# DLRM interaction kernel: 16 by-hand gathers, w_tri loaded amid SP's first rows, the last output in two halves

## What is computed

```python
x = jax.nn.relu(dense_features @ W0 + b0)
x = jax.nn.relu(x @ W1 + b1)
dense_out = jax.nn.relu(x @ W2 + b2)
emb = jax.vmap(lambda t, idx: t[idx], in_axes=(0, 1), out_axes=1)(tables, sparse_features)
gram = jnp.einsum('bid,bjd->bij', emb, emb)
interact = gram[:, TRIU_I, TRIU_J]
features = jnp.concatenate([dense_out, interact], axis=1)
return features @ Wt + bt
```

## Time and profile before

| what | us |
|---|---|
| median of 3 runs | 523.09 |
| lowest and highest | 522.91, 523.14 |
| the profiled execution's own time | 523.56 |
| its span, first to last instruction | 521.5 |
| POOL busy | 381.4 |
| PE busy | 304.8 |
| DVE busy | 246.6 |
| ACT busy | 19.2 |

### The profile page before, as it was taken

The page is one execution under the profiler, slowest core; times in us unless marked ns, Lnnn a source line. Parts: engine busy times, 40 slices in busy tenths (PEclk is TensorE's granted clock), DMA queues, the critical chain, the costliest instruction groups (busy, mean ns, idle before and its releaser), DMA issues.

```text
span 521.5 us, 8547 instructions
## 1 busy us (share of the span) xinstructions
PE 304.8 (58%) x1752; PEld 242.1 (46%) x1752; DVE 246.6 (47%) x635; ACT 19.2 (4%) x53; POOL 381.4 (73%) x409
## 2 busy tenths in 40 slices
PE   2814761668576776857577083270734683814697
PEld 1504551547454664746456062250623562713585
DVE  4255533436566374555736345162461865331532
ACT  2000000000000000000000000000000000210312
POOL 5777777777777777777777777777777777777770
PEclk9965575776796776767778557585575757665769
DMA  7212224232232222322222222232222222121110
GB/s 112 28 29 28 31 47 94 30 37 29 38 29 38 29 30 37 31 37 30 38 29 29 37 29 38 29 38 28 31 36 28 40 27 37 27 37 26 38 35 14
DMA packets 24945, 18.74 MB, mean 36 GB/s; under 512 B 14615, under 2 KB 18425, under 8 KB 24876
## 3 DMA queue, kind: packets, MB, share of 16 engines
q0 software_dynamic: 12864, 13.20, 17.8%
q1 hardware_dynamic: 6100, 2.46, 4.8%
q10 hardware_dynamic: 5930, 2.55, 4.4%
HBM read 15.25 MB, written 2.10 MB: 33 GB/s over the span
## 4 chain that ended last, share of the span: by engine, by line
POOL 38%; issue 16%; PE 16%; DVE 13%; SPq 10%; DMA 5%; POOLq 0%; DVEq 0%
POOL emb L321 34%; DVE gram L235 8%; SPq L251 6%; PE mlp_ps L584 6%; PE gram_ps L659 5%; POOL emb L345 4%; DMA w_tri<-in_L_rec_Wt_dram 3%; DVE h L422 2%; PE mlp_ps L671 2%; DVE embT L212 2%; SPq L245 2%; SPq L285 1%; DMA w_gram<-w_tri 1%; PE rowsT_ps L635 1%; PE mlp_ps L591 1%
## 5 line engine op out<-in xcount | busy, mean ns | idle before, releaser
L321 POOL DMA_INDIRECT emb<-in_L_rec_tables_dram,row_idx x376 | 356.0, 947 | 117.7 <-issue 114.2
L235 DVE COPY gram<-gram_ps 32x96 f32<-32x96 f32 x464 | 150.3, 324 | 98.2 <-PE gram_ps L659 92.4
L635 PE MATMUL rowsT_ps<-ident,emb 128*128 128x128 f32 x188 | 36.9, 330 | 122.5 <-DMA emb<-in_L_rec_tables_dram,row_idx 109.7
L659 PE MATMUL gram_ps<-embT 64*128 64x100 f32 x1024 | 92.9, 350 | 23.0 <-DVE gram L235 10.4
L659 PEld LDWEIGHTS gram_ps<-embT 64*128 64x128 f32 x1024 | 86.9, 259 | 32.3 <-issue 32.3
L635 PEld LDWEIGHTS rowsT_ps<-ident,emb 128*128 128x128 f32 x188 | 24.4, 164 | 134.2 <-issue 133.4
L212 DVE COPY embT<-rowsT_ps 128x512 f32<-128x512 f32 (+1 forms) x60 | 47.7, 851 | 74.7 <-PE rowsT_ps L635 74.3
L671 PE MATMUL mlp_ps<-w_gram,gram 128*128 128x256 f32 x224 | 70.6, 483 | 0.1
L584 PE MATMUL mlp_ps<-h,w_sb 128*128 128x256 f32 x128 | 48.7, 562 | 34.3 <-DVE h L422 34.3
L671 PEld LDWEIGHTS mlp_ps<-w_gram,gram 128*128 128x128 f32 x224 | 58.5, 262 | 13.6 <-issue 0.5
L584 PEld LDWEIGHTS mlp_ps<-h,w_sb 128*128 128x128 f32 x128 | 37.3, 299 | 46.7 <-DVE h L422 38.5
(11 more groups left out here) (38 smaller groups left out, 45.0 us busy)
## 6 DMA issues: line engine op xcount, KB each, us to landing
by_hand<-in_L_rec_tables_dram SPq DMA_DIRECT2D x896, 0.2 KB
by_hand<-in_L_rec_tables_dram ACTq DMA_DIRECT2D x896, 0.2 KB
emb<-in_L_rec_tables_dram,row_idx POOLq DMA_INDIRECT x378, 3.4
out_dram<-out_sb ACTq DMA_DIRECT2D x16, 128.0 KB, 8.7
w_gram<-w_tri SPq DMA_DIRECT2D x3, 192.0 KB
w_sb<-in_L_rec_W_dram SPq DMA_DIRECT2D x1, 512.0 KB
emb<-in_L_rec_tables_dram,last_idx POOLq DMA_INDIRECT x24, 2.5
raw_idx<-n_r_sparse_features_dram SPq DMA_DIRECT2D x2, 182.0 KB, 4.2
```

The costliest lines, as they stand in the source:

```text
L235: last = copy(by_quad[FP * g:FP * (g + 1), t0:NS, :, half * HG:(half + 1) * HG, s], gram_ps[FP * s:FP * (s + 1), :, :, src:src + SQ * (NS ...
L321: nc.gpsimd.indirect_dma_start(emb[:, m % PR, k, u, :], None, tables_v[:, :], bass.IndirectOffsetOnAxis(ap=row_idx[:, u, m, k:k + 1], axis=0),
L635: last = nc.tensor.transpose(rowsT_ps[c % 2][:, k - ks.start, :, :], rows.rearrange("p u e -> p (u e)"), ident[:, :])
L659: last = nc.tensor.matmul(gram_ps[:, u, a, 0:SQ * (F - 1)], samples.rearrange("p s f -> p (s f)"), samples[:, :, 1:F], start=True, stop=True)
```

## The change

Pair 14 is added to BY_HAND, so eight pairs have 16 gathers by hand in all. SP loads w_tri after the first 64 of pair 2's rows instead of after all 128. SP_ONLY is empty, so the code that asks for it does nothing.

The last pair's output is made in two halves of 64 samples. `gram_evac` lays the last pair's halves side by side, and the last round of the dense layers writes its output in the same order, in two relu instructions. `top_first_half` forms the first half's output ahead of `last_transposes(3)`; DVE copies it out and ACT stores it in two transfers. `top_last_half` forms the second half's: slots 4 to 6 go into PSUM partitions 64 to 127 of one buffer, the dense part and slots 0 to 3 into partitions 0 to 63 of the other, in turn. ACT copies the former out, DVE adds the two, SP and ACT store 32 rows each. The spare products are set anew: four ahead of `last_transposes(2)`, two ahead of `last_transposes(5)`, five after the last Gram products.

```diff
-    BY_HAND = [2, 4, 5, 7, 9, 10, 12]
+    BY_HAND = [2, 4, 5, 7, 9, 10, 12, 14]
+    SP_ONLY = []
...
-    SPARE = [4, 3, 5]
+    SPARE = [4, 2, 5]
+    SPLIT = 4
     def gathered(m, c):
-        return 2 * len([k for k in CHUNKS[c] if k != HAND_K or m not in BY_HAND])
+        return 2 * len([k for k in CHUNKS[c] if k != HAND_K or m not in BY_HAND]) + (c == LAST and m in SP_ONLY)
...
+    out_last = out.rearrange("(u h r t) o -> h u r t o", u=2, h=2, t=NP)
...
         def gram_evac(copy, blocks, m, half):
-            by_quad = gram[:, m % 2, :, :].rearrange("p t (u a s) -> p t u a s", u=2, s=SQ)
+            if m == LAST_PAIR:
+                by_quad = gram[:, m % 2, :, half * US:(half + 1) * US].rearrange("p t (u a s) -> p t u a s", u=2, s=SQ)
+            else:
+                by_quad = gram[:, m % 2, :, :].rearrange("p t (u h a s) -> p t h u a s", u=2, h=2, s=SQ)[:, :, half]
             for s, g in blocks:
...
-                    by_quad[FP * g:FP * (g + 1), t0:NS, :, half * HG:(half + 1) * HG, s],
+                    by_quad[FP * g:FP * (g + 1), t0:NS, :, :, s],
...
             sp.dma_start(wd_sb[H2:H2 + 1, :], bt.rearrange("(a n) -> a n", a=1)).then_inc(w_top_in, 16)
             sp.wait_ge(hand_idx_ready, 1)
-            fetch_rows(sp, 0, BY_HAND[0], 0, P)
+            fetch_rows(sp, 0, BY_HAND[0], 0, US)
             sp.wait_ge(tri_zeroed, 1)
             for i in range(F - 1):
                 n = F - 1 - i
                 sp.dma_start(w_tri[i:i + 1, i:F - 1, :],
                              wt[tri_row(i):tri_row(i) + n, :].rearrange("(a j) n -> a j n", a=1)).then_inc(tri_in, 16)
+            fetch_rows(sp, 0, BY_HAND[0], US, P)
             sp.wait_ge(tri_in, 16 * (F - 1))
             for g in range(SQ):
                 t0 = first_slot(g)
...
                              w_tri[:, col(t0, g) - 1:F - 1:SQ, :]).then_inc(w_top_in, 16)
             for m in BY_HAND[1:]:
                 fetch_rows(sp, 0, m, 0, P)
-            for q in range(2):
-                sp.wait_ge(stored[q], 16 * ROUNDS)
+            sp.wait_ge(out_ready[1], ROUNDS + 1)
+            sp.dma_start(out_last[1, 0, :, LAST_PAIR, :], tail_sb[0:HS, 1, :]).then_inc(stored[1], 16)
+            sp.wait_ge(stored[0], 16 * ROUNDS)
+            sp.wait_ge(stored[1], 16 * (ROUNDS + 3))
         @block.gpsimd
         def _(pool):
...
             def l2_evac(r):
                 dve.wait_ge(l2_in_psum, r + 1)
-                relu(h2[0:H2, r, :], mlp_ps[1][0:H2, 0:RS], b2_sb[:, 0:1]).then_inc(h2_ready, 1)
+                if r < ROUNDS - 1:
+                    relu(h2[0:H2, r, :], mlp_ps[1][0:H2, 0:RS], b2_sb[:, 0:1]).then_inc(h2_ready, 1)
+                    return
+                relu(h2[0:H2, r, 0:P], mlp_ps[1][0:H2, 0:P], b2_sb[:, 0:1])
+                relu(h2[0:H2, r, P:RS].rearrange("p (h u s) -> p h u s", h=2, u=2),
+                     mlp_ps[1][0:H2, P:RS].rearrange("p (u h s) -> p h u s", h=2, u=2), b2_sb[:, 0:1]
+                     ).then_inc(h2_ready, 1)
...
             gram_blocks(LAST_PAIR, 0)
             out_evac(LAST_PAIR - 1)
+            dve.wait_ge(top_in_psum[1], ROUNDS)
+            dve.wait_ge(stored[1], 16 * (ROUNDS - 1))
+            nc.vector.tensor_copy(out_sb[0:US, 1, :], mlp_ps[1][0:US, 0:NO]).then_inc(out_ready[1], 1)
             for i in range(HALF_DONE[0], HALF_DONE[1]):
...
             gram_blocks(LAST_PAIR, 1)
-            out_evac(LAST_PAIR)
+            dve.wait_ge(top_in_psum[1], ROUNDS + 1)
+            dve.wait_ge(tail_part_ready, 1)
+            nc.vector.tensor_tensor(tail_sb[:, 1, :], mlp_ps[1][0:US, 0:NO], tail_sb[:, 0, :], ALU.add
+                                    ).then_inc(out_ready[1], 1)
         @block.scalar
         def _(act):
...
                     gram_evac(nc.scalar.copy, ACT_BLOCKS, m, half).then_inc(gram_tail_act, 1)
                     if half == 0 and m == LAST_PAIR:
                         store(m - 1)
+                        act.wait_ge(out_ready[1], ROUNDS)
+                        for u in range(2):
+                            act.dma_start(out_last[0, u, :, LAST_PAIR, :], out_sb[u * HS:(u + 1) * HS, 1, :]).then_inc(
+                                stored[1], 16)
                 if m < LAST_PAIR:
                     store(m - 1)
-            store(LAST_PAIR)
+            act.wait_ge(tail_top_in_psum, 1)
+            nc.scalar.copy(tail_sb[:, 0, :], mlp_ps[0][US:P, 0:NO]).then_inc(tail_part_ready, 1)
+            act.wait_ge(out_ready[1], ROUNDS + 1)
+            act.dma_start(out_last[1, 1, :, LAST_PAIR, :], tail_sb[HS:US, 1, :]).then_inc(stored[1], 16)
         @block.tensor
         def _(pe):
...
-            def spare(n):
-                pe.wait_ge(out_ready[(LAST_PAIR - 1) % 2], (LAST_PAIR - 1) // 2 + 1)
+            def spare(n, m):
+                pe.wait_ge(out_ready[m % 2], m // 2 + 1)
                 for _ in range(n):
-                    nc.tensor.matmul(mlp_ps[(LAST_PAIR - 1) % 2][:, 0:NO], ident[:, :], w_gram[:, 0, :], start=True, stop=True)
+                    nc.tensor.matmul(mlp_ps[m % 2][:, 0:NO], ident[:, :], w_gram[:, 0, :], start=True, stop=True)
...
                                             start=False, stop=(t == NS - 1))
                 last.then_inc(top_in_psum[q], 1)
+            def half_of(samples, half):
+                return samples[:, half * US:(half + 1) * US]
+            def top_first_half():
+                nc.tensor.matmul(mlp_ps[1][0:US, 0:NO], half_of(h2[:, ROUNDS - 1, P:2 * P], 0), wd_sb[:, :],
+                                 start=True, stop=False)
+                blocks_out(2 * LAST_PAIR + 1)
+                for t in range(NS):
+                    last = nc.tensor.matmul(mlp_ps[1][0:US, 0:NO], half_of(gram[:, 1, t, :], 0), w_gram[:, t, :],
+                                            start=False, stop=(t == NS - 1))
+                last.then_inc(top_in_psum[1], 1)
+            def top_last_half():
+                pe.wait_ge(out_ready[1], ROUNDS)
+                nc.tensor.matmul(mlp_ps[1][0:US, 0:NO], half_of(h2[:, ROUNDS - 1, P:2 * P], 1), wd_sb[:, :],
+                                 start=True, stop=False)
+                blocks_out(2 * LAST_PAIR + 2)
+                for t in range(SPLIT):
+                    if SPLIT + t < NS:
+                        last = nc.tensor.matmul(mlp_ps[0][US:P, 0:NO], half_of(gram[:, 1, SPLIT + t, :], 1),
+                                                w_gram[:, SPLIT + t, :], start=(t == 0), stop=(SPLIT + t == NS - 1))
+                        if SPLIT + t == NS - 1:
+                            last.then_inc(tail_top_in_psum, 1)
+                    last = nc.tensor.matmul(mlp_ps[1][0:US, 0:NO], half_of(gram[:, 1, t, :], 1), w_gram[:, t, :],
+                                            start=False, stop=(t == SPLIT - 1))
+                last.then_inc(top_in_psum[1], 1)
...
-            for i in range(HALF_DONE[0]):
-                last_transposes(i)
+            last_transposes(0)
+            last_transposes(1)
+            spare(SPARE[0], LAST_PAIR - 3)
+            last_transposes(2)
             gram_products(LAST_PAIR, 0)
             top(LAST_PAIR - 1)
+            top_first_half()
             last_transposes(3)
-            spare(SPARE[0])
             last_transposes(4)
-            spare(SPARE[1])
+            spare(SPARE[1], LAST_PAIR - 1)
             last_transposes(5)
             gram_products(LAST_PAIR, 1)
-            spare(SPARE[2])
-            top(LAST_PAIR)
+            spare(SPARE[2], LAST_PAIR - 1)
+            top_last_half()
```

More of the change, by code:

```diff
@@ L151, in bass_dlrm_forward @@
         out_sb = sb("out_sb", [P, 2, NO])
+        tail_sb = sb("tail_sb", [US, 2, NO])
         rowsT_ps = [pb(f"rowsT_ps_{i}", [P, 4, 2, US]) for i in range(2)]
@@ L198, in bass_dlrm_forward @@
         out_ready = [sem(f"out_ready_{q}") for q in range(2)]
+        tail_top_in_psum = sem("tail_top_in_psum")
+        tail_part_ready = sem("tail_part_ready")
         stored = [sem(f"stored_{q}") for q in range(2)]
@@ L317, in gather @@
                     for k in ks:
+                        if k == HAND_K and m in SP_ONLY:
+                            nc.gpsimd.indirect_dma_start(
+                                by_hand[:, BY_HAND.index(m), 1, :], None, tables_v[:, :],
+                                bass.IndirectOffsetOnAxis(ap=row_idx[:, 1, m, k:k + 1], axis=0),
+                            ).then_inc(rows_in[m % PR][c], 16)
                         if k == HAND_K and m in BY_HAND:
@@ L524, in store @@
                 act.dma_start(out_v[:, m:m + 1, :], out_sb[:, m % 2:m % 2 + 1, :]).then_inc(stored[m % 2], 16)
-            pieces = [(m, c0) for m in BY_HAND for c0 in range(0, P, LOADED)]
+            pieces = [(m, c0) for m in BY_HAND if m not in SP_ONLY for c0 in range(0, P, LOADED)]
             act.wait_ge(hand_idx_ready, 1)
@@ L626, in transposes @@
                     if own:
-                        for u in range(2):
```

(4 more changed lines are left out.)

## The result

The kernel after takes 519.76 us in the median of four runs (519.16, 519.27, 520.25 and 521.84); before, beside it, took 523.12. The ratio is 0.9946 with a 95% interval of 0.9932 to 0.9961: half a per cent faster, which is clear of the noise. The two medians lie 3.4 us apart; the ratio stands for 2.8 us. The forecast was 520.4 in a range of 519.2 to 522.4, and a gain of 2.7. The runs lie wider apart than those of before (2.7 us against 0.4).

The account below looks back on a forecast made before the run. POOL's count of gathers and what follows the last were taken as the whole time. Span 521.5 less 2.50 and 1.06, plus 0.85 for the clock, gave 518.8; 2.7 off the 523.09 median gave 520.4, range 519.2 to 522.4.

Parts of the forecast that it names:

- Two gathers less: On POOL: 400 gathers instead of 402 at 1.25 us each, the last one 2.50 us sooner, at 504.53.
- The halves side by side: In the last slots: records of two column halves run beside each other, 2.20 us instead of 3.26, 1.06 saved.
- The clock: On PE: a fall at about the last Gram products in most executions, 1.71 us whole, taken as 0.85; chance 0.36.
- (c): Rival on PE: clock falls ahead of the last products and stays low through ten spare records, +2.6 us, time 522.1; chance 0.15.
- (a): Rival on PE: the clock holds at its high level, span 517.94, time 519.5; chance 0.24.
- The first half's output ahead of last_transposes(3): On PE: 16 records, 3.4 us, put ahead of those transposes without delaying the last products, 1.7 us to spare.
- F: On PE: the time when the first half's output ends, forecast at 503.7; the last products could follow 2.7 us later.
- The sum of halves: On DVE: adding the two column halves takes 0.42 us, as the copy it replaces, bounds 0.35 to 0.50.
- w_tri: Loads amid SP's rows of pair 2: PE's 11.2 us wait for w_gram goes, but the end gains nothing.
- the rows are wanted at 477 and land by 442. Cost: nothing: Pair 14's 128 rows each on SP and ACT land in time; ACT's end near 439, with 10 us to spare.
- slack 1.7 us, cost nothing: Before the last products: PE is ready at 506.4, the last rows allow them at 508.11, so the early output costs nothing.
- rival (e): On PE: the first half's products become the path; low clock throughout gives +6.8 us, time 526.3; chance 0.05.

Follow-up runs that it names:

- e6_tail: After with pair 14 taken out of BY_HAND again, so POOL makes 402 gathers and the new tail stays; 522.99 us, ratio 0.9994 to before.
- e3_hold: After with five instead of two spare products ahead of last_transposes(5); 520.92 us, ratio 0.9968 to before.
- e2_sequence: e3_hold with all seven last slots in sequence in one half and a plain copy by DVE; 522.41 us, ratio 0.9993 to before.
- a2_after: After measured again without any edit, on another chip; 521.15 us over 7 runs, ratio 0.9963 to before.
- e11_odd: After with pair 14's u = 1 rows gathered by POOL again (401 gathers, 1920 rows); 520.68 us, ratio 0.9964 to before.
- e5_tri: After with SP loading w_tri behind all 128 rows of pair 2, as in before; 520.71 us, ratio 0.9958 to before.
- e10_split: After with each row described as 2 x 128 bytes, though the rows went out whole; 519.93 us, ratio 0.9951 to before.
- e4_fall: After with no spare products ahead of last_transposes(5) instead of two; 522.21 us, ratio 0.9984 to before.
- e9_spares: After with six and four spare products ahead of last_transposes(2) and last_transposes(5) instead of four and two; 520.64 us, ratio 0.9946 to before.
- e1_gathers: Before with pair 14 added to BY_HAND and nothing else; 522.91 us, ratio 1.0003 to before.

## Why the prediction was right

**The sum.** Three measurements of after give ratios of 0.9946, 0.9963 and 0.9951 and medians 3.4, 2.1 and 2.8 us below before; the forecast had 2.7. The terms, one by one:

- Two gathers less: 2.50 forecast. The last gather goes out at 503.90 and 504.07, 3.1 and 3.0 us sooner. Two gathers are 2.50; the rest is the step from gather to gather, which is 1.2504 us in the profile of after against 1.2521 in that of before, 0.7 us over 400 gathers. It differs as much where nothing of POOL was changed: e6_tail, with 402 gathers, has its last at 506.05, 1.0 us sooner than before.
- The halves side by side: 1.06 forecast from 3.26 to 2.20, and 1.94 measured at the high clock (e3_hold), 1.3 saved against sequence; e2_sequence shows 1.5 in the median.
- The clock: +0.85 in the middle. After's profile has the whole 1.71 and the spare products' overrun of 0.9 behind it; a2_after has nothing. The forecast put its main chance on a fall at the time of the products, and the profiles show its rivals (c) and (a). What the clock costs in the mean of all executions no run shows, as one execution of each was profiled.
- The first half's output ahead of last_transposes(3): F forecast 503.7, measured 503.2. F + 2.7 for the products holds where F comes last: 506.52 + 2.72 in e11_odd, 507.00 + 2.73 in e5_tri, 504.91 + 2.72 in e10_split. (The pieces that the prediction lists for it make 2.4.)
- The sum of halves takes 0.42, and the end comes 2.13 behind the last stores. Both as forecast.
- w_tri: nothing for the end, and nothing found within the 1.6 us that e5_tri can tell.

So the mechanism held in its main lines: POOL ends two gathers sooner, and the last slots are shorter. That the total came within a microsecond is partly luck. The gathers and the halves gave some 0.8 us more than forecast in the profiles, and delays of PE that the prediction had put at nothing took time back in some executions.

**The steps that failed.** First, "the rows are wanted at 477 and land by 442. Cost: nothing". ACT issued its last rows at 447.9, not 439: 128 rows and two stores took 58.6 us from 389.3 on and not 49.9. In the timeline ACT pauses 2.4 us ahead of a piece of 32 rows to load its addresses (434.90 to 437.35 is one) and 3.2 us where a store lies between, 11.3 us for the four pieces; the 96 issues of the earlier trace rows hold two such pauses, 4.9 us. The rows themselves were issued at 11.4 us a piece instead of 10.6. Of the 10 us to spare one was left. More than that, the step looked at when the rows by hand are issued, and not at what they do to POOL's own rows. Their lag, 20 us already in before but over by 419, now reaches pair 13 and half of pair 14. The rows of before showed it, had I asked the view of the gathers' line for landings: a maximum of 12.1 us, and 20.2 chunk by chunk, against 2.8.

Second, "slack 1.7 us, cost nothing". It supposed the first half's products at 494.6 and a high clock from 494 on. In after's profile, a2_after, e3_hold and e4_fall POOL sets the last products, as forecast. In others PE's own order does, 0.6 to 2.5 us behind POOL, in one of two ways. In e10_split, e9_spares and e5_tri the stage of pairs 13 and 14 ends late: the clock rose only at 487.0, 487.8 and 489.2 (483.4 in after), and the first half's products start at 495.62, 496.38 and 497.72; with pair 13 16 us late, PE has no wait for rows there in which to catch up. (Two of e9_spares' products, 0.9 us, are its own added spares.) In e6_tail and e11_odd, where pair 13 comes 17 and 11 us sooner, the clock was low from 495.8 to 502.6 and from 495.2 to 502.1, amid the first half's Gram and top. The path of rival (e) thus occurs, in one of the three profiled executions of after (e10_split among them) and in four other kernels, but not at the 6.8 us of its full price.

Third, that the gathers and the tail add up. Alone neither the gathers (e1_gathers) nor the tail (e6_tail) give a gain that can be told. The prediction took POOL's count as the time; it is the time only while PE and DVE stay under it, and by the profile of e1_gathers, where the last gather allows the last products at 507.4 and they start at 511.30, they don't with two gathers less and the old tail.

**What stays open.** Why the clock rises and falls at other times in each execution, and how much of the spread among equal kernels (up to 5 us) it makes. Why the lag stops growing at some 20 us. And where the rows by hand queue. The Trainium skill (DMA: Bandwidth & Descriptors, Why a DMA increments its semaphore by 16 and not by 1) says that a transfer from SP or ACT whose outer dimension can't be divided over several engines runs on a single engine, the lowest-numbered one, while a gather of POOL's counts all sixteen as they finish. The trace agrees as far as it goes: one of a gather's sixteen updates is late and the others are not, and the delay is 0.22 us a row, as of one queue. A shortage that all sixteen share would not leave fifteen of them on time. The trace doesn't name the engines, so that the rows and the late part meet on the same one is inferred; the split in two pieces, which was to test it, didn't reach the transfers.

## What to carry to other kernels

Work that is moved from a full queue to an empty one can come back as latency: look at the time from issue to landing of what stays, through the whole kernel, not only at whether the moved transfers are in time. Before a count on the bounding engine is turned into time, work out how far the next engine is below it at its slow clock as well as its fast one; here two gathers alone gave no gain that could be told, and 2 to 3 us together with the new tail. Where a clock's level differs from execution to execution, give the sum at either level, and expect the median between them.

## What the runs showed of the hardware that was not expected

Small transfers issued by SP and ACT, one row of 256 bytes each, delay the landing of POOL's gathers: from 2.8 us to a steady 20 us, at a cost of 0.22 us a row until the backlog is gone, while the mean busy share of the sixteen transfer engines stays near 0.2. Only one of a gather's sixteen semaphore updates is late, the others come within 2.8 us; the gather counts as landed with the last. POOL's step from gather to gather stays at 1.25 us all the while. The lag stopped growing at 19 to 22 us in every kernel, even where rows by hand went on for 180 us more (after, from 264 to 441). Products into PSUM partitions 0 to 63 and 64 to 127 from two column halves start pairwise within 0.04 us of each other, also where the half changes with every record.
